# A gated cross-attention and mixture-of-experts kernel: the third tile's transposes ahead of the value projection

## What is computed

```python
q = l @ Wq;  k, v = split(concat([norm(ctx), l]) @ Wkv)      # l = norm(norm(x)); 333 keys a batch
w = softmax(q @ k.T / 8)          # per head: 256 x 333
x = x + tanh(g_xattn) * ((w @ v) @ Wo)
x = x + tanh(g_ffn) * (top2_of_16_experts(norm(x)) + shared(norm(x)))
```

## Time and profile before

| | |
|---|---|
| median of 3 runs | 1320.49 us (1318.95 to 1324.10) |
| the profiled execution, its own time | 1321.79 us |
| its span, first to last instruction | 1320.1 us |
| mean granted TensorE clock | 0.991 |
| TensorE matmuls | 1245.5 us busy, 94% |
| VectorE, ScalarE, GpSimd | 67%, 59%, 35% busy |
| chain that ended last | PE 80%, DVE 11%, issue 5%, ACT 2% |

### The profile page before, as it was taken

One profiled execution on the slowest core, in us unless ns is written; L12 is line 12 of the kernel. 1 busy time (PEld: TensorE's weight loads), 2 busy tenths in 40 slices (PEclk: granted clock), 3 DMA queues, 4 the chain that ended last, 5 costly groups with the idle time before them and its releaser, 6 DMA issues.

```text
span 1320.1 us, 28357 instructions
## 1 busy us (share of the span) xinstructions
PE 1245.5 (94%) x8982; PEld 1016.7 (77%) x8982; DVE 878.5 (67%) x2646; ACT 782.6 (59%) x2278; POOL 459.4 (35%) x638
## 2 busy tenths in 40 slices
PE   3899999999999999999999998999999989999995
PEld 2788787878787878787878787878788878787774
DVE  5666677777777777777777777777776655434554
ACT  3766666666666666666656666666666656454442
POOL 2422323333333333333323333333333322444554
PEclk9999999999999999999999999999999989999998
DMA  8910000000000000000000000000000070445666
GB/s 258 318 32 1 3 1 3 18 4 18 4 18 5 18 8 14 5 18 8 14 5 18 3 18 5 18 7 14 9 9 9 12 193 33 123 127 170 195 209 203
DMA packets 61839, 70.90 MB, mean 54 GB/s; under 512 B 7072, under 2 KB 56176, under 8 KB 61680
## 3 DMA queue, kind: packets, MB, share of 16 engines
q1 hardware_dynamic: 54192, 48.91, 12.8%
q0 software_dynamic: 6912, 18.95, 4.0%
q10 hardware_dynamic: 576, 1.05, 0.2%
HBM read 35.19 MB, written 33.70 MB: 52 GB/s over the span
## 4 chain that ended last, share of the span: by engine, by line
PE 80%; DVE 11%; issue 5%; ACT 2%; DMA 1%; POOL 1%; DVEq 0%; SPq 0%; POOLq 0%; ACTq 0%
PE pj L1357 25%; PE ov L1422 11%; PE st L1403 10%; PE st L1387 9%; PE yb L1484 6%; PE st L560 5%; PE pj L513 3%; PE ov L579 3%; DVE neg_max L1309 2%; PE st L550 2%; DVE PT L1341 1%; PE ov L1013 1%; PE pj L516 1%; DVE Q_hl L1329 1%; PE yb L527 1%
## 5 line engine op out<-in xcount | busy, mean ns | idle before, releaser
L1161 ACT ACTIVATE probs<-st,neg_max 128x333 f32<-128x333 f32 x512 | 268.5, 537 | 268.0 <-DVE neg_max L1309 257.7
L1106 POOL TENSOR_TENSOR probs<-probs,inv_sum 128x333 f32<-128x333 f32 x128 | 94.5, 738 | 677.0 <-DVE inv_sum L1320 677.0
L1309 DVE TENSOR_REDUCE neg_max<-st 128x2 f32<-128x666 f32 x256 | 205.8, 845 | 139.9 <-PE st L1403 139.9
L1387 PE MATMUL st<-ident,probs 128*128 128x128 f32 (+1 forms) x1536 | 203.7, 272 | 0.0
L1422 PE MATMUL ov<-PT,V 128*64 128x256 f32 (+1 forms) x1536 | 196.6, 391 | 0.0
L1387 PEld LDWEIGHTS st<-ident,probs 128*128 128x128 f32 (+1 forms) x1536 | 182.6, 143 | 16.1 <-issue 0.8
L1403 PE MATMUL st<-K_hl,Q_hl 64*128 64x334 f32 x1536 | 152.9, 330 | 18.7 <-issue 9.8
L1357 PE MATMUL pj<-wkv,lT 128*128 128x512 f32 (+1 forms) x576 | 158.4, 410 | 11.6 <-DVE Q_hl L1329 11.2
L1341 DVE COPY PT<-st 128x512 f32<-128x512 f32 x256 | 163.6, 681 | 0.0
L1422 PEld LDWEIGHTS ov<-PT,V 128*64 128x64 f32 (+1 forms) x1536 | 99.7, 137 | 64.1 <-issue 27.5
L1403 PEld LDWEIGHTS st<-K_hl,Q_hl 64*128 64x128 f32 x1536 | 118.6, 187 | 38.3 <-issue 26.0
(11 more groups left out here) (177 smaller groups left out, 1797.1 us busy)
## 6 DMA issues: line engine op xcount, KB each, us to landing
slots_x<-zeros SPq DMA_DIRECT2D x10, 1032.0 KB, 12.8
V<-slots_x SPq DMA_DIRECT2D x80, 129.0 KB
yg<-routed_y SPq DMA_DIRECT2D x32, 256.0 KB
out<-X SPq DMA_DIRECT2D x32, 128.0 KB
X<-in_x SPq DMA_DIRECT2D x2, 1024.0 KB, 14.0
w_gu<-in_L_ffn_expert_gate_w SPq DMA_DIRECT2D x2, 960.0 KB, 9.1
w_gu<-in_L_ffn_expert_up_w SPq DMA_DIRECT2D x2, 960.0 KB, 10.4
w_dn<-in_L_ffn_expert_down_w SPq DMA_DIRECT2D x1, 1920.0 KB, 12.7
```

The costliest lines, as they stand in the source:

```text
L1106: pool.tensor_tensor(probs[:, v, 0, 0:SKV], probs[:, v, 0, 0:SKV], inv_sum[:, v, 0:1].to_broadcast([P, SKV]), ALU.mult).then_inc(normed, 1)
L1161: nc.scalar.activation(probs[:, v, i, 0:SKV], st_bank(i)[:, 0:SKV], ACT.Exp, bias=neg_max[:, v, i:i + 1], accum_out=sums[:, v, i:i + 1]).t ...
L1309: nc.vector.tensor_reduce(neg_max[:, v, 2 * i:2 * i + 2], st[i][:, :, 0:SKV], AX.X, ALU.max, negate=True).then_inc(maxed, 1)
L1387: last = nc.tensor.transpose(st_bank(kt)[0:kn, at:at + P], probs[:, v, i, k0:k0 + kn], ident[:])
```

## The change

It moves two things in every step that has values (places 0, 1, 2, 4, 5, 6; 96 of 128 steps). On TensorE `turned(2)` goes ahead of the values' matmuls, right behind `turned(0)` and `turned(1)`. On ScalarE the copy of the third tile goes ahead of the copy of values. No instruction, wait or buffer is added or removed.

```diff
@@ scalar, step
+            if has(LAG_T):
+                m, v = PAIRS * bb + u - LAG_T, (u - LAG_T) % 2
+                kn = KT[2][1]
+                act.wait_ge(pt_full, NKT * m + 3)
+                copy(PT[0:kn, v, 2, :], st_bank(2)[0:kn, :], ACT.Copy).then_inc(pt_hi, 1)
             if p in V_STEPS and has(0):
                 kt, half = V_STEPS[p] % NKT, V_STEPS[p] // NKT
                 kn = KT[kt][1]
                 n, bank, free, _ = filled("V", len(V_STEPS), bb, len(V_STEPS) * (u // PAIRS) + V_STEPS[p])
                 act.wait_ge(pj_full, n + 1)
                 copy(V[0:kn, kt, half * 512:(half + 1) * 512], bank[0:kn, :], ACT.Copy).then_inc(free, 1)
-            if has(LAG_T):
-                m, v = PAIRS * bb + u - LAG_T, (u - LAG_T) % 2
-                kn = KT[2][1]
-                act.wait_ge(pt_full, NKT * m + 3)
-                copy(PT[0:kn, v, 2, :], st_bank(2)[0:kn, :], ACT.Copy).then_inc(pt_hi, 1)
@@ tensor, step
                 turned(0)
                 turned(1)
+                turned(2)
             if p in V_STEPS and has(0):
...
                 split3(bank[0:kn, :], lambda a, k: lT[:, w, a, k, k0:k0 + kn],
                        lambda a, k: wkv[:, a, k, INNER + half * 512:INNER + (half + 1) * 512]).then_inc(pj_full, 1)
-            if has(LAG_T):
-                turned(2)
```

## The result

| | before | after |
|---|---|---|
| median of the runs | 1320.41 us (4 runs, 1318.95 to 1324.10) | 1305.65 us (4 runs, 1304.46 to 1306.41) |
| profiled execution | 1321.79 us | 1306.41 us |
| its span, mean granted clock | 1320.1 us, 0.991 | 1304.7 us, 0.987 |

The kernel is faster by 14.8 us: the ratio is 0.9882, with an interval of 0.9869 to 0.9895. The forecast was 18.7 us, so the median lies 3.9 us above it.

A forecast was written before the change was run, and what follows sets the result against it. TensorE was taken to bound the kernel, its values waiting for VectorE's low part of the queries. 5.4 + 5.0 + 3.4 + 2.2 + 3.2 - 0.5 = 18.7 us off 1320.5 gave 1301.8 us, range 1297 to 1310.

The forecast's parts named there:

- Place 2: 5.4 us: Place 2 of each batch: 12 batches gain 0.43 us each, keeping a wait of about 0.19; with step 2, 5.4 us.
- place 6: 5.0 us: Place 6 of each batch: excess of 0.43 us in ten batches, 0.24 in three, little elsewhere; gain 5.0 us.
- Places 1 and 5: These places of each batch: excess of 0.08 us in some 28 steps, gain 2.2 us.
- Place 0: Place 0 of each batch: excess of 0.21 us in nine batches, 0.38 in four; 3.4 us, ScalarE's gain counted separately.
- Four transposes are worth 0.43 us: TensorE, ahead of the values: twelve transposes take 1.22 us, eight 0.79, so a step gains up to 0.43 us.
- The rivals with 0.36 us and with the page's rate: Cheaper transposes on TensorE: four cost only 0.36 us, about 1304 us, or by the skill page about 1305; chance 0.05.
- ScalarE's copy: Third tile's copy to `PT` ends earlier, so scores come 0.16 us sooner, mostly at place 0: 20 x 0.16 = 3.2 us.
- The scatter: Place 3: VectorE may wait longer for GpSimd's scatter, with 0.05 us of cover left; 0 to 3.4 us lost, 0.5 taken.
- VectorE did not take the wait's place: Rival: gains at places 2 and 6 return as waits for `PT`, 7.9 us lost, 1309.7 us; chance 0.13.
- the wait did not move with the values: Rival: TensorE's holdup follows its matmul order, not the queries, so only ScalarE's part comes: 1317 us; chance 0.04.
- no transpose waited for an exponential: Rival: the third tile's transposes wait for the step's third exponential, 96 steps lose 0.3 us each, 1331 us; chance 0.02.
- The step that failed: Behind the attention: the experts, on the same chain, only move forward; no separate gain or loss was given.

The follow-up runs named there:

- the queries first: VectorE computes the queries' low part ahead of the attention output's low part: 1312.27 us in the kernel before, 1305.45 us on top of the changed kernel.

## Why the prediction was right, and where it was short

The forecast was 1301.8 us with a range of 1297 to 1310 and faster at 0.92; it became 1305.65 us and faster. Point by point:

- **The bound was read rightly.** The values waited for VectorE's low part of the queries. The change takes the wait from 15.6 us to 2.4, and computing that part earlier takes two thirds of it away, without touching TensorE. The bank's time stayed where it was against the scores, as the prediction had it: at place 2 the low part of the queries starts 5.27 us behind the step's scores before and 5.28 after.
- **The terms of the steps held.** "Place 2: 5.4 us" measured 5.4, "place 6: 5.0 us" measured 5.0. The wait that was to stay at place 2 is there, 10 times named, 0.2 us each. Places 1 and 5 gave 3.2 us instead of 2.2, since a step gave 0.10 and not 0.08 us, and the first and last ones 0.2 to 0.3. Place 0 was to give 3.4 us with 3.2 from ScalarE, some 2.0 of both at the edges and a little in single steps; outside the edges it gave 4.1.
- **Four transposes are worth 0.43 us.** The steps at places 2 and 6 that had a longer wait shrank by 0.40 to 0.47, 0.43 on average. The rivals with 0.36 us and with the page's rate are out: twelve transposes take 1.23 us to the next matmul's start and eight 0.79, so one more takes about 108 ns. The prediction's 102 ns is too small, since the matmul behind the last one starts early. Its prices for the two rivals were a little high: 22 capped steps and four partly capped ones lose 1.6 us at 0.36 and 2.7 us at 0.32, not about 2 and 3 to 4. The 81 ns of the Trainium skill ("TensorE: Matmul & The Clock Gate", "Back-to-back issue gap") is not what these fp32 transposes show.
- **ScalarE's copy.** The 0.16 us at place 0 came. But as a term of its own the 3.2 us were wrongly assigned: the copies alone give 1.4 us, and the transposes alone lose 15.6. The total holds because both moves were costed together; the split between the two terms is not what either move gives by itself.
- **The scatter.** 0.5 us was set aside, nothing was needed; place 3 takes what it took. The cover of 0.05 us did not come out so: in step 51 VectorE's wait for the scatter grew from 0.72 to 0.96 us, by 0.24 and not by 0.43, and 0.24 of the 0.48 are left. In step 67 none is left, and there the step gets longer with the queries first.
- **The rivals.** VectorE did not take the wait's place (12 waits for `PT` as before, 4.2 us), the wait did not move with the values, and no transpose waited for an exponential.
- **The step that failed** stands in the sum: "The experts come behind the attention on the same chain and only move forward", and with it that all outside the counted steps stands still. The steps gained 17.8 us (the forecast had some 16.7 for them); the start lost 1.8 where nothing was expected, and the eight steps at the loop's edges lost 1.6 where 2.0 of gain were. The second pair of traces has 17.5, 1.6 and 0.4. Most of this is TensorE's clock: 1.6 us at the start and 2.9 us behind two edges. The profile before had what was needed to ask: four waits for issue of up to 2.6 us, and 0.72 in two windows behind them. The mean of 0.991, which the prediction called nearly full, hides them. The tail's 1.0 us in the first pair is within what two traces of one kernel differ by. Without the edges the medians differ by 17.2 us and the steps by 17.6; that this comes so near the forecast is in part luck, since place 6 then gives 3.2 us and not 5.0.

Why the clock falls more often with the new order is open. The longer idle time of the start isn't needed for it: 1.66 us ahead of the scores had the fall in the run with step 2 in the old order, 1.67 and 1.68 us had not before the change and with ScalarE's half, and 1.95 us had it in one run and not in another. But it may make the fall more frequent there: five of five traces at 2.1 us against one of six at 1.7. At the edges it can't be this, since the idle time is the same before and after (9.8 and 9.9 us in four). That the new order leaves TensorE in another state or phase when the idle time begins is possible, and no run here tests it.

## What to carry to other kernels

When two engines each run in a fixed order, a move on one is judged together with the order of its reader on the other: one half lost 15.6 us here, the other gave 1.4, both gave 14.8. Moved work hides no more of a wait than its own length and no more than the wait, so cost the move by the smaller of the two, step by step, and keep what remains. And look at the granted clock by windows wherever TensorE stands idle as long as here (1.7 to 2.7 us), at the edges of a loop above all: with 15 us at stake, three more stretches at the lower clock took some 4.5 us of it by the traces. Writing the loop out gave 10, though some 5 us of what it gained in the attention were lost again behind it.

## What was not expected of the hardware

- Behind an idle time of 2.1 to 2.7 us at the loop's edge the clock is granted at 1.2 GHz for a stretch (0.72 on average over 6 us) or not lowered at all, and the same kernel does it at other edges in another execution. One such stretch costs 1.2 to 1.5 us (the step behind the edge takes 9.58 against 8.39 us before, and 9.57 against 8.05 with the queries first).
- An edge of the hardware loop costs TensorE 2.1 to 2.7 us although everything it waits for is there. The Trainium skill states for the instruction fetch ("Runtime: NRT & Kernel Launch", "Instruction fetch mechanics") that a taken branch whose target lies outside the pages at hand breaks the sequential prefetch and stalls the engine until the target's page has come. The trace agrees so far as the idle time has no releaser but issue and vanishes when the loop is written out, for 11.0 us at four edges before the change and 14.2 after, the lower clock with it; that it is the fetch, no row here shows.
- Written out, the two programs take 5.0 and 5.5 us longer behind the last scores, in the traces. Why stayed open.
- Written out, VectorE's chain up to the queries is 0.1 to 0.2 us shorter at places 2 and 6 (at place 6 the low part of the queries starts 4.86 us behind the step's scores instead of 5.06), so that place 6 has only 0.22 us of excess in all batches. That is why the change gains 3.2 us there instead of 5.0. Why a loop should lengthen that chain stayed open.
